# Neighbour sums of the MoE rounds: unit slots summed by accumulating gathers into a ring of 16 unit sums

## The reference

```python
h = x @ W_in + b_in                                     # 256 wide
for l in range(3):                                      # the three MoE rounds
    agg = segment_sum(h[src], dst, N) / deg
    logits = concat([h, agg]) @ router_W[l] + router_b[l]
    vals, idx = top_k(logits, 2);  gates = softmax(vals) # spread over 8 experts
    weak = relu(agg @ weak_W[l] + weak_b[l])             # 4 experts
    strong = relu(agg @ strong_W1[l] + b1) @ strong_W2[l] + b2   # 4 experts
    h = h + sigmoid(h @ conf_W[l] + conf_b[l]) * sum_e gates_e * expert_e
x = layernorm(x + h @ W_out + b_out)
# then two attention rounds (GAT): for each node a softmax over its edges of
# leaky_relu(a_s[src] + a_d[dst]), and the weighted sum of h[src], 132 columns wide
x = layernorm(x + gat2(elu(gat1(x))))
```

## Time and profile before

| | us |
|---|---|
| time, median of 3 runs | 6931.53 |
| lowest and highest | 6931.01, 6934.34 |
| the profiled execution, its span | 9249.5 |
| prologue up to the first gather of a MoE round | 518 |
| each MoE round's gather stream, as profiled | 1760, 1762, 1763 |
| each attention round's gather stream, as profiled | 1376, 1389 |
| between the streams, and behind the last | 114, 115, 302, 68, 82 |

### The profile page before, as it was taken

One profiled execution on the slowest core, in us unless ns is written; L12 is line 12 of the kernel. 1 busy time (PEld: TensorE's weight loads), 2 busy tenths in 40 slices (PEclk: granted clock), 3 DMA queues, 4 the chain that ended last, 5 costly groups with the idle time before them and its releaser, 6 DMA issues. The chain is left out here.

```text
span 9249.5 us, 91514 instructions
## 1 busy us (share of the span) xinstructions
PE 4191.8 (45%) x21235; PEld 3360.2 (36%) x21235; DVE 4614.2 (50%) x9920; ACT 1371.9 (15%) x4985; POOL 4726.6 (51%) x4956
## 2 busy tenths in 40 slices
PE   6136677676477677763666777772000000000000
PEld 3035566565355555653555565551000000000000
DVE  8225554554255555552455545524555553555554
ACT  2012212221112122221122222221000000000000
POOL 1644444445454444444444444425666666666665
PEclk9567888888688787886788888865555555555555
DMA  1132222223222222232222222211222222222222
GB/s 46 30 89 64 69 69 63 67 66 71 84 71 67 64 68 68 64 64 91 65 68 62 68 65 68 64 22 43 45 46 46 46 45 48 45 46 46 45 45 42
DMA packets 270134, 542.64 MB, mean 59 GB/s; under 512 B 125302, under 2 KB 141881, under 8 KB 269961
## 3 DMA queue, kind: packets, MB, share of 16 engines
q0 software_dynamic: 202832, 511.64, 23.7%
q1 hardware_dynamic: 67260, 30.51, 1.2%
HBM read 510.76 MB, written 31.05 MB: 59 GB/s over the span
## 5 line engine op out<-in xcount | busy, mean ns | idle before, releaser
L477 POOL DMA_INDIRECT ring<-hidden_tab,stage x2688 | 2550.6, 949 | 2811.6 <-DVE part L696 1815.5
L477 POOL DMA_INDIRECT ring<-gat_tab,stage x1792 | 1696.4, 947 | 1073.1 <-issue 543.9
L696 DVE TENSOR_REDUCE part<-ring 128x256 f32 x657 | 1262.1, 1921 | 335.7 <-issue 259.2
L1243 PE MATMUL ps_w1a<-agg_t,wbuf 128*128 128x128 f32 x4704 | 821.0, 335 | 764.7 <-issue 558.3
L1243 PE MATMUL ps_w1b<-agg_t,wbuf 128*128 128x128 f32 x4704 | 838.3, 330 | 618.5 <-issue 500.0
L1284 PE MATMUL ps_moe<-wbuf,strong 128*128 128x256 f32 x4704 | 1057.3, 383 | 0.0
L1243 PEld LDWEIGHTS ps_w1a<-agg_t,wbuf 128*128 128x128 f32 x4704 | 758.4, 247 | 787.6 <-issue 564.9
L1243 PEld LDWEIGHTS ps_w1b<-agg_t,wbuf 128*128 128x128 f32 x4704 | 760.3, 241 | 696.9 <-issue 575.9
L1284 PEld LDWEIGHTS ps_moe<-wbuf,strong 128*128 128x128 f32 x4704 | 883.5, 190 | 163.8 <-issue 48.1
L738 DVE TENSOR_SCALAR gate_n<-ex 128x2 f32<-128x2 f32 x147 | 25.3, 172 | 1783.6 <-ACT ex L1003 1696.0
L870 DVE TENSOR_REDUCE gacc<-strong 128x132 f32<-128x660 f32 x438 | 575.9, 1315 | 23.4 <-issue 15.6
(11 more groups left out here) (273 smaller groups left out, 5444.0 us busy)
## 6 DMA issues: line engine op xcount, KB each, us to landing
ring<-hidden_tab,stage POOLq DMA_INDIRECT x2688
ring<-gat_tab,stage POOLq DMA_INDIRECT x1792
hidden_tab<-h_res SPq DMA_DIRECT2D x49, 128.0 KB, 1.7
wbuf<-in_L_gnn_strong_W SPq DMA_DIRECT2D x6, 1024.0 KB
wbuf<-in_L_gnn_strong_W SPq DMA_DIRECT2D x12, 512.0 KB
stage<-slot_tab SPq DMA_DIRECT2D x280, 8.0 KB
wbuf<-in_L_gnn_weak_W SPq DMA_DIRECT2D x6, 512.0 KB
slot_tab<-wbuf SPq DMA_DIRECT2D x1, 1584.0 KB, 6.0
```

The source lines that it names most:

```text
L477: pool.indirect_dma_start(out=ring[:, b, 0:width], out_offset=None, in_=table, in_offset=bass.IndirectOffsetOnAxis(ap=stage[:, b * 2 // RI ...
L696: nc.vector.tensor_reduce(part[:], ring[:, bass.ds((q % UNITS) * SLOTS, SLOTS), :].rearrange("p s n -> p n s"), AX.X, ALU.add).then_inc(ri ...
L1243: last = mm(ps_w1[s % 2][:, c * P:(c + 1) * P], w1_w[:, k, s, c * P:(c + 1) * P], agg_t[odd][:, k * P:(k + 1) * P], start=k == 0, stop=k == 1)
```

## The change

The sum over the four slots of a unit is taken from DVE and given to the DMA engines, in the MoE rounds alone.

- `ring` holds 16 unit sums in a MoE round (one row of 256 floats for each unit) in place of 8 units of four slots. In the attention rounds the same memory is a ring of 64 slots of 136 floats (`gat_ring`), 16 units. The tile is 34 rows wide in place of 32. `hist` and `zeros`, which the prologue alone uses, move into `wbuf`.
- `sum_units` takes the place of the slot loop in the MoE rounds. It goes over half of the ring, 8 units and 32 gathers, at a time. In a first pass (j = 0) it gathers the first slot of each of the 8 units. In three more passes (j = 1, 2, 3) it gathers slot j of each unit with `compute_op=ALU.add`, so that the DMA adds the fetched row to the one in the ring. Gathers go out in pairs of two units. Since an accumulating gather needs the one before it in place, each pair of passes 1 to 3 waits (`landed`) until the pair of the pass before has landed on the same two units.
- In the last pass a pair of units is complete, and `arrived` counts it. The wait for this stands ahead of the next pair: three times within the last pass, and once ahead of the next half's first gather.
- DVE adds the finished unit sum to the group's sum (line 744 of the changed kernel). The reduction and `part` are gone there, and one `drain` with them.
- `early(r)` and the two semaphores for the last two units set the counts for units that arrive two at a time. SP stages halves of 32 slots in place of 16. A round has 224 units and 896 gathers as before.

```diff
-RING = 32
+RING = 64
...
-        ring = sb("ring", [P, RING, H])
+        ring = sb("ring", [P, RING * GW // H, H])
...
+                def landed(u, i, count):
+                    pool.wait_ge(gathered[u], i * (16 * SLOTS) + (16 * count + (16 * SLOTS if u >= UNITS - 2 else 0)))
...
+                def sum_units(i, half):
+                    pool.wait_ge(staged[half], i * 16 + 16)
+                    pool.sem_inc(half_begun, 1)
+                    for j in range(SLOTS):
+                        for u in range(0, UNITS // 2, 2):
+                            n = half * UNITS // 2 + u
+                            if j == 0:
+                                if u == 0:
+                                    for k in range(2):
+                                        landed(n - 2 + k if half else UNITS - 2 + k, i, SLOTS if half else 0)
+                                    pool.sem_inc(arrived, 2)
+                                pool.wait_ge(ring_free, i * UNITS + (n + 2))
+                                pool.sem_inc(unit_open, 1)
+                                for k in range(2):
+                                    into(ring[:, n + k, :], half, (u + k) * SLOTS).then_inc(gathered[n + k], 16)
+                                continue
+                            if j == SLOTS - 1 and u:
+                                for k in range(2):
+                                    landed(n - 2 + k, i, SLOTS)
+                                pool.sem_inc(arrived, 2)
+                            for k in range(2):
+                                landed(n + k, i, j)
+                            pool.sem_inc(unit_open, 1)
+                            for k in range(2):
+                                pool.indirect_dma_start(
+                                    out=ring[:, n + k, :], out_offset=None, in_=table,
+                                    in_offset=bass.IndirectOffsetOnAxis(ap=stage[:, half, (u + k) * SLOTS + j:(u + k) * SLOTS + j + 1], axis=0),
+                                    compute_op=ALU.add).then_inc(gathered[n + k], 16)
...
-                    nc.vector.tensor_reduce(part[:], ring[:, bass.ds((q % UNITS) * SLOTS, SLOTS), :].rearrange("p s n -> p n s"),
-                                            AX.X, ALU.add).then_inc(ring_free, 1)
-                    dve.drain()
-                    nc.vector.tensor_tensor(acc, acc, part[:], ALU.add)
+                    nc.vector.tensor_tensor(acc, acc, ring[:, bass.ds(q % UNITS, 1), :].rearrange("p a n -> p (a n)"), ALU.add)\
+                        .then_inc(ring_free, 1)
```

More of the change, by code:

```diff
@@ L464, in _, with into @@
                 table = hidden_tab[r] if r < LAYERS else gat_tab[r - LAYERS]
-                width = H if r < LAYERS else GW
-                with pool.Fori(bodies * r, bodies * (r + 1)) as i:
+                def landed(u, i, count):
+                    pool.wait_ge(gathered[u], i * (16 * SLOTS) + (16 * count + (16 * SLOTS if u >= UNITS - 2 else 0)))
+                def into(tile, half, k):
+                    return pool.indirect_dma_start(
+                        out=tile, out_offset=None, in_=table,
+                        in_offset=bass.IndirectOffsetOnAxis(ap=stage[:, half, k:k + 1], axis=0))
@@ L467, in _, with raw_slots @@
+                def raw_slots(i):
                     for b in range(RING):
@@ L839, in rows_of @@
                 def rows_of(unit):
-                    return ring[:, bass.ds(unit % UNITS * SLOTS, SLOTS), 0:GW]
+                    return gat_ring[:, bass.ds(unit % UNITS * SLOTS, SLOTS), :]
                 def score_unit(q):
-                    dve.wait_ge(arrived, total * LAYERS + q + (r + 2))
+                    dve.wait_ge(arrived, total * LAYERS + q + (early(r) + 1))
                     nc.vector.tensor_tensor(score[:, 0:SLOTS, :], rows_of(q)[:, :, GW - HEADS:GW],
```

40 lines of the change are left out of this document (25 added, 15 removed).

## The result

| | before | changed |
|---|---|---|
| time, median of 3 runs, us | 6931.53 | 8938.06 |
| lowest and highest | 6931.01, 6934.34 | 8932.56, 8938.63 |
| ratio, with its 95% interval | | 1.2889 (1.2866 to 1.2912) |
| the profiled execution, its span | 9249.5 | 8931.0 |

The prediction said 7710 us (7150 to 8300). The direction is right and the size is not: 8938 lies 638 us above the range. The kernel before runs at 6931 us in some groups of runs and at 9240 to 9380 us in others, on one and the same chip too and with or without a profile, and the profiled execution shown ahead of the prediction was of the second kind, that of the changed kernel of the first.

The account below looks back on a forecast made before the run. The prediction took POOL's pace of issuing gathers to bound the unprofiled kernel. Its terms, 6931.5 + 924 for new stops - 143 for old landing waits, the rest at 0, gave 7712, called 7710 us, range 7150 to 8300.

Parts of the forecast that it names:

- The reading: POOL's queue in the kernel before: unprofiled, the pace at which gathers are issued, 1.25 us each, bounds the time.
- The subtraction 9249.5 - 2195 = 7054 > 6931.5: Profiled span less POOL's 2195 us of waits for DVE already exceeds the unprofiled time, so the profiler makes nearly all.
- (a): DVE's reduction in MoE rounds goes: 1262 us of work beside the gather stream, taken as worth 0, 150 for the range.
- (b): New stops in MoE rounds, POOL waiting for the two gathers directly ahead: 336 at 2.75 us, +924 us.
- (c): Old landing waits ahead of MoE gathers go, 128 units held 1.1 us each: -143 us.
- (d): Passes 1 to 3, waits for the same unit's gather eight back: 10.0 us against slowest landing 5.63, so nothing.
- (f): Waits for `ring_free`, DVE having read a ring unit before its reuse: 0; attention rounds 0 to -60 us, taken as 0.
- (e): The 2016 MoE gathers that accumulate: taken at 0 extra, upper bound 0.242 us each, 488 us.
- 1: Rival: accumulates cost POOL or the DMA engines 0.24 us more each, 8200 us in all; chance 0.17.
- 2: Rival: the new stops are cheap, 1.15 us each, 7175 us in all; chance 0.15.
- 3: Rival: unprofiled POOL issues gathers faster, say at 1.0 us, and DVE's chain bound MoE rounds: 6650 us; chance 0.07.
- My check for (a): Profiled MoE rounds may well get shorter, since their 590 us of waits for DVE are the profiler's.

Follow-up runs that it names:

- before_look: The kernel before, unchanged, run again for a profile: 6931.24 us in nine runs, profiled execution spanning 6932.4 us.
- no_stop_b: Changed kernel without its 336 stops, landings waited for later: 7957.17 us beside 6929; as no_stop, 8539.3 us beside 9288.7.
- paced: Kernel before with two POOL memsets and two drains ahead of three in four MoE gathers: 12909.9 us beside 9246.9.
- paced_light: Kernel before with one POOL memset and no drain ahead of three in four MoE gathers: 7324.41 us, ratio 1.0557.
- late_wait: Kernel before, waiting for a unit's landing six gathers behind its last instead of two; four runs: ratios 1.0137, 1.0126, 1.0138, 1.0115.

## Why the prediction was wrong, step by step

The sum with measured terms, from before_look to the changed kernel: 6932.4 + 1196 (accumulates) + 984 (336 stops of 2.93) - 184 (waits gone) = 8928 us, and the span is 8931.0.

- **The reading, "the kernel runs at the pace at which POOL issues gathers": right**, for a reason that was half wrong. The subtraction 9249.5 - 2195 = 7054 > 6931.5 pointed the right way: the 6931 us have little room for waits for DVE, and before_look has 40 us of them. It was not the profiler that made the others but an execution of another course.
- **(a) DVE's reduction, worth 0: right.** 40 us at the most were to be had, and they went into the term for the waits.
- **(b) Stops, 336 x 2.75 = +924: right in size**; 2.92 each in full time, 981 us. The number of 4.0 us from a gather to the next one is 1.25 + 2.59 = 3.84 for plain gathers and 1.85 + 2.93 = 4.78 for accumulating ones, whose landing takes longer, so that the forecast of 4.0 fits the plain ones. The row of 4.59 us was the useful one. The Trainium skill's formula (DMA: Bandwidth & Descriptors, Anatomy of one DMA — SWDGE (gpsimd) path) was worked out to an estimated 1.35 us a stop; the trace does not agree, with 2.59 for a plain one.
- **(c) Waits gone, -143: nearly right**, -184. In before_look the MoE gathers have 1041.7 us ahead of them, 2688 x 0.305 = 820 of it ordinary. The other 222 are 31 ahead of the three rounds' first gathers, 29 of DVE, and some 162 at third slots of a unit, where the wait for the landing stands, though the profile puts down most of these to "<-issue". no_stop_b shows the change: 3555 + 1197 - 4568 = 184 us, of the 191 that landings and DVE had.
- **(d) and (f), nothing: right.** 399.8 us ahead of the accumulates "<-issue" are 1312 times the ordinary 0.30; gaps and attention streams stayed, and of the waits for `ring_free` (99.9 us, 56 times) 26 fall on first gathers of a half, where a stop is anyway, and the others are no longer than the ordinary 0.30.
- **(e) The accumulate, taken at 0 with 0.242 us as upper bound: this is the step that failed.** It is 0.593 us, 2.5 times the bound, 1196 us in all. Two things went wrong. First, the upper end came from the longest plain gather, and a spread among plain gathers bounds nothing that an added operation does: no row of the trace had an add in it. Second, the argument for 0, that the write of descriptors depends on the number of rows, was worked out on plain gathers alone, and an add makes another transfer of the same rows. The DMA queue and the packet sizes show it, first of the kernel before (before_look), then of the changed one:

```profile
DMA packets 270134, 542.64 MB, mean 78 GB/s; under 512 B 125302, under 2 KB 141881, under 8 KB 269961
q0 software_dynamic: 202832, 511.64, 31.2%
```

```profile
DMA packets 443514, 542.66 MB, mean 61 GB/s; under 512 B 105143, under 2 KB 379770, under 8 KB 443338
q0 software_dynamic: 396368, 511.64, 33.9%
```

The queue's bytes are equal to the digit and its packets are 193536 more, 96 for each of the 2016 accumulates. From 2 to 8 KB there are 64512 packets fewer (32 for each accumulate), from 512 B to 2 KB there are 258048 more (128 for each): a plain gather moves its 128 rows in 32 packets of 4 KB, an accumulating one in 128 of 1 KB, a packet for each row. That the POOL instruction is longer because it writes more descriptors is the likely reading; the profile counts packets and not descriptors, and no run tries it apart. The Trainium skill (Collectives: The Full Stack, The bandwidth ceiling) has an add in the DMA engine make two source reads with two read descriptors; by this the prediction estimated 0.47 us, and the measured 0.593 is far nearer to it than to the bound from the rows. The nearness may be chance, since the packets of a gather grew fourfold and not by half. The estimate stood in the text and had no weight in the sum or the range.

**The rivals.** 1 was the right mechanism at under half its price: with 0.593 in place of 0.242 its own sum gives 7712 + 1196 = 8908. 2 and 3 fell: a stop costs 2.93 us on average, and POOL's pace is the same 1.25 us in runs of 6931 us. My check for (a), that the profiled MoE rounds may get shorter, misled too: the profile of after has them at 1851 us against 1760, and only at 1185 are they comparable. Its sign for the reading, a gain in the profile beside a loss in the runs, did come out (9249.5 to 8931.0 us beside 6931.5 to 8938), but by luck: the two profiles are of two kinds of execution. And neither condition that it named for being wrong, another pace without the profiler or a stop under 1 us, came about; the term at nothing was not among them.

No version here beats the kernel before where that takes 6931 us. By no_stop_b, an order with no stop still loses 1028 us: the idea fails on POOL's time, which the kernel had least of.

## What to carry to other kernels

Ask first which engine writes the descriptors. If the queue that issues the gathers is the bound, moving arithmetic from an engine with room into those gathers can't win, however much work it takes off the other. Where an edit adds an operation that no row of the trace shows, don't bound it by the spread of similar ones: let the range reach what a second one of the same would cost (here 0.95 us, of which 0.59 came true). And when the profiled span and the runs differ by a third, the profile may be of another kind of execution: compare the sum of pure instruction time with the runs before trusting any wait, and lay an experiment's time beside the kernel before of the same kind only.

## What the runs showed of the hardware

- A gather of 128 rows of 1 KB with an add keeps POOL for 1.540 us, against 0.947 plain (2016 rows of the changed kernel, 2688 of before_look). It moves them in 128 packets of 1 KB, a plain one in 32 of 4 KB. It has its data in place later too: a stop behind it costs 2.93 us, behind a plain one 2.59.
- POOL's 0.30 us between two gathers is not all lost: a memset of 0.38 us put there delays the next gather by 0.24 us. A memset with a drain behind it, though, cost about 1.4 us each.
- PE can stall with nothing to wait for: 558 and 500 us ahead of the matmuls of ps_w1a and ps_w1b in the kernel before at 9249.5 us, none at 6932. One and the same chip gives either time (paced stands beside 9247 us, paced_light beside 6934). At 9249.5 us PE's granted clock in a MoE stream is 0.80 of full speed, at 6932 us 0.95. The stalls are long where plain gathers are dense (1050 us ahead of ps_w1b in late_wait), shorter with accumulating ones (98 in no_stop), and absent in paced. Their cause is open.
